# Graph 0's two aggregations in plain fp32, its loads split over two queues

## The reference

```python
def _L0(x, adj):  return adj @ (x @ weight) + bias
def _L1(x, adj):                 # first 25 nodes only, five node groups
    for g, idx in enumerate(GROUPS):
        h = graph_conv(x[:, idx], adj[:, idx][:, :, idx], W1[g], b1[g])      # relu(norm_adj @ (x @ W) + b)
        fused[:, idx] += norm_w[g] * graph_conv(h, adj_g, W2[g], b2[g])
def _L2(x, adj):                 # h = x @ W.T + b; e, f = h @ a1, h @ a2
    u = adj * exp(e[:, :, None] + f[:, None, :] + a_b)
    return (u / u.sum(2)) @ h
x = layernorm(x + _L0(x, adj))
x = layernorm(x + _L1(x, adj))
x = layernorm(x + _L2(x, adj))
x = layernorm(x + _L3(x, adj))   # convolutions, message passing with exp(-dist), a gated unit
```

## Time and profile before

| | us |
|---|---|
| median of 3 runs | 573.02 |
| lowest, highest | 571.81, 573.85 |
| the profiled execution, its own time | 571.94 |
| its span in the trace | 570.2 |
| mean granted clock of TensorE | 0.998 |
| busy: PE, DVE, ACT, POOL | 550.7, 477.9, 399.0, 218.5 |

### The profile page before, as it was taken

How to read it: one execution, slowest core, us unless ns; L and a number is a source line. 1 busy time by engine, 2 the same in 40 slices (tenths; PEclk the granted TensorE clock), 3 DMA queues, 4 the chain that set the end, 5 groups by cost and what they waited for, 6 DMA issues and landing times.

```text
span 570.2 us, 12148 instructions
## 1 busy us (share of the span) xinstructions
PE 550.7 (97%) x3639; PEld 486.2 (85%) x3639; DVE 477.9 (84%) x1768; ACT 399.0 (70%) x844; POOL 218.5 (38%) x213
## 2 busy tenths in 40 slices
PE   6889999999999999999999999999999999999994
PEld 6777898989889898989898898989898988989684
DVE  3887778898888989888888889898888888898665
ACT  2477576777787868687777878686777778786452
POOL 3312125263534434352635344343526353442010
PEclk9999999999999999999999999999999999999999
DMA  7980060020020303030200203030302002000000
GB/s 182 327 281 1 1 202 1 2 79 36 20 93 0 111 0 111 0 111 0 80 32 24 87 0 111 0 111 0 111 0 89 23 23 88 2 20 20 2 20 18
DMA packets 33301, 34.46 MB, mean 60 GB/s; under 512 B 1663, under 2 KB 22531, under 8 KB 33146
## 3 DMA queue, kind: packets, MB, share of 16 engines
q1 hardware_dynamic: 32930, 33.99, 18.8%
q10 hardware_dynamic: 344, 0.15, 0.1%
HBM read 29.74 MB, written 4.39 MB: 60 GB/s over the span
## 4 chain that ended last, share of the span: by engine, by line
PE 86%; DVE 1%; ACT 1%; issue 0%; POOLq 0%; POOL 0%; DVEq 0%
PE bank L265 14%; PE bank L267 14%; PE bank L266 14%; PE pair L265 6%; PE pair L267 6%; PE pair L266 6%; PE bank L1685 5%; PE bank L1696 3%; PE bank L1789 2%; PE pair L1845 2%; PE pair L1777 2%; PE bank L1880 2%; PE bank L1881 2%; PE bank L1884 2%; PE bank L1750 1%; PE bank L1860 1%
## 5 line engine op out<-in xcount | busy, mean ns | idle before, releaser
L1173 POOL TENSOR_TENSOR rs<-ve,neg_half 128x4 f32<-128x4 f32 (+1 forms) x60 | 55.3, 921 | 136.1 <-DVE ve L1409 101.2
L1207 POOL TENSOR_TENSOR P_lo<-P,P_hi 128x512 fp32r<-128x512 f32 x56 | 81.9, 1482 | 49.0 <-ACT P_hi L1246 49.0
L265 PE MATMUL bank<-cd_hi,w_hi 128*128 128x256 f32 x272 | 77.2, 284 | 0.0
L266 PE MATMUL bank<-cd_lo,w_hi 128*128 128x256 f32 x272 | 76.5, 281 | 0.0
L267 PE MATMUL bank<-cd_hi,w_lo 128*128 128x256 f32 x272 | 76.2, 280 | 0.0
L1444 DVE TENSOR_TENSOR P<-bank,aT 128x512 f32<-128x512 f32 x64 | 41.1, 684 | 16.7 <-ACT bank L1232 16.6
L265 PE MATMUL pair<-aT_hi,x_hi 128*128 128x512 f32 x128 | 52.2, 408 | 1.5 <-DVE x_lo L809 1.3
L266 PEld LDWEIGHTS bank<-cd_lo,w_hi 128*128 128x128 f32 x272 | 51.2, 188 | 1.6
L265 PEld LDWEIGHTS bank<-cd_hi,w_hi 128*128 128x128 f32 x272 | 51.3, 189 | 1.4
L267 PEld LDWEIGHTS bank<-cd_hi,w_lo 128*128 128x128 f32 x272 | 51.4, 189 | 0.0
L267 PE MATMUL pair<-aT_hi,x_lo 128*128 128x512 f32 x128 | 50.5, 394 | 0.0
(11 more groups left out here) (384 smaller groups left out, 1695.7 us busy)
## 6 DMA issues: line engine op xcount, KB each, us to landing
adj_nat<-in_adj_dram SPq DMA_DIRECT2D x16, 1024.0 KB, 5.9
x_nat<-in_x_dram SPq DMA_DIRECT2D x16, 256.0 KB, 2.9
xt<-in_x_dram SPq DMA_DIRECT2D x3, 1280.0 KB, 12.2
out_dram<-y_out SPq DMA_DIRECT2D x15, 256.0 KB, 2.3
hw<-in_L_gnn_W_dram SPq DMA_DIRECT2D x2, 640.0 KB, 8.4
xt<-in_L_gnn_conv_w_dram SPq DMA_DIRECT2D x1, 1088.0 KB, 6.8
aT<-in_adj_dram SPq DMA_DIRECT2D x5, 96.0 KB
nat_ih<-in_L_gnn_w_ih_dram SPq DMA_DIRECT2D x1, 384.0 KB, 6.1
```

Of the source, the lines that this page charges most:

```text
L265: nc.tensor.matmul(o, lh, rh, start=start, stop=False)
L266: nc.tensor.matmul(o, lh, rl, start=False, stop=False)
L1173: g.tensor_tensor(rs[i][:, 0:n], ve[i][:, 0:n], neg_half[:, 0:n], ALU.pow).then_inc(po_rs[i], 1)
L1207: g.tensor_tensor(P_lo[:, mc, :], P[:, mc, :], f(P_hi[:, mc, :]), ALU.subtract).then_inc(po_Plo[mc], 1)
```

## The change

Both aggregations of graph 0 take unsplit fp32 operands in one product for each chunk instead of three passes; copies, rests and their waits go (semaphores that the loop counts on are raised by hand). Adjacency 0 comes in two halves of two chunks, and TensorE transposes the first half of every block, then the second. The own-row loads wait for the first half. `xt` 0 to 2, `hw1` and `hw2` are issued by ScalarE, the first two after the first half has landed, the last three behind the four adjacency copies; four vectors move to SyncE, and SyncE's loads of own rows of x wait for `xt` 1. On TensorE the output product comes ahead of `transpose_rows`, and the latter are spread out. On VectorE, own-row masks of tile 1 move behind y1's statistics, those of tile 2 behind the normalisation.

```diff
@@ sync
-                sp.dma_start(adj_nat[0][:, :, :], adj_v[0]).then_inc(adj_in[0], 16)
+                sp.dma_start(adj_nat[0][:, 0:2, :], adj_v[0][:, 0:2, :]).then_inc(q_adj0, 16)
+                sp.dma_start(adj_nat[0][:, 2:NC, :], adj_v[0][:, 2:NC, :]).then_inc(adj_in[0], 16)
+                sp.wait_ge(q_adj0, 16)
...
-                sp.wait_ge(adj_in[0], 16)
-                x_tile(0)
-                sp.dma_start(hw1 ...)
+                for row, name, n in ((G2, ...), (BB2, ...), (M2, ...), (V2, ...)):
+                    sp.dma_start(vrows[row:row + n, :], ...)
...
-                sp.dma_start(hw2 ...)
-                x_tile(1)
-                x_tile(2)
+                sp.wait_ge(q_xr[1], 16)
@@ scalar
-                act.wait_ge(x_in[0], 16)
-                s.activation(x_hi[:, :, :], x_nat[0][:, :, :], ACT.Identity).then_inc(ac_xhi, 1)
+                act.sem_inc(ac_xhi, 1)
...
+                act.wait_ge(q_adj0, 16)
+                x_tile(0)
+                act.dma_start(hw1[:, :, :], ...).then_inc(q_h1, 16)
                 for mc in range(NC):
                     act.wait_ge(pe_aT[mc], 1)
-                    s.activation(aT_hi[:, mc, :], bank[mc][:, :], ACT.Identity).then_inc(q_aThi, 1)
+                    s.activation(aT[0][:, mc, :], bank[mc][:, :], ACT.Identity).then_inc(ac_aT[mc], 1)
+                act.dma_start(hw2[:, :, :, :], ...).then_inc(q_h2, 16)
+                x_tile(1)
+                x_tile(2)
                 act.wait_ge(pe_agg1, 1)
                 s.activation(agg_sb[:, :], AG_BANK[:, :], ACT.Identity).then_inc(ac_agg1, 1)
                 copy_rows(0)
+                act.wait_ge(q_cols, 1)
+                s.activation(cols[:, :], bank[7][:, 0:NROWS], ACT.Identity).then_inc(q_colsb, 1)
                 copy_rows(1)
-                for mc in (2, 0, 1, 3):
...
-                    act.wait_ge(dv_aTlo[mc], 1)
-                    s.activation(aT[0][:, mc, :], bank[mc][:, :], ACT.Identity).then_inc(ac_aT[mc], 1)
...
-                    s.activation(x_hi[:, c, 1:D], x2[:, c, 1:D], ACT.Identity, scale=pef[:, 1, c:c + 1])...
+                    s.activation(x3[:, c, 1:D], x2[:, c, 1:D], ACT.Identity, scale=pef[:, 1, c:c + 1])...
@@ vector
-                v.tensor_tensor(x_lo[:, :, :], x_nat[0][:, :, :], f(x_hi[:, :, :]), ALU.subtract).then_inc(x_rest, 1)
+                dve.sem_inc(x_rest, 1)
                 for mc in range(NC):
-                    rest_of_adjacency(mc)
-                dve.wait_ge(adj_in[0], 16)
+                    dve.sem_inc(dv_aTlo[mc], 1)
+                dve.wait_ge(q_adj0, 16)
...
                 degrees(NODES, 0, NG, 1)
-                dve.wait_ge(q_adjP, 32 * PJ)
-                v.tensor_tensor(AB[0:R, 1:NT, :], ...).then_inc(q_A1, 1)
-                hold(dve, q_A1, 3)
-                mask_blocks(1)
                 inverse_degrees(NODES, 0, NG, 1)
...
-                mask_blocks(2)
+                dve.wait_ge(q_adjP, 32 * PJ)
+                v.tensor_tensor(AB[0:R, 1:NT, :], ...).then_inc(q_A1, 1)
+                hold(dve, q_A1, 3)
+                mask_blocks(1)
...
+                mask_blocks(2)
                 mask_blocks(3).then_inc(q_A5, 1)
...
-                v.tensor_copy(x_hi[:, :, 0], pef[:, 1, :]).then_inc(dv_pfh, 1)
-                dve.wait_ge(dv_pfh, 1)
-                v.tensor_tensor(x_lo[:, :, 0], pef[:, 1, :], f(x_hi[:, :, 0]), ALU.subtract).then_inc(dv_pf, 1)
+                v.tensor_copy(x3[:, :, 0], pef[:, 1, :]).then_inc(dv_pf, 1)
+                dve.sem_inc(dv_pfh, 1)
                 for c in range(NC):
-                    hold(dve, ac_xs[c], 1)
-                    v.scalar_tensor_tensor(x_lo[:, c, 1:D], ...).then_inc(dv_xs[c], 1)
+                    dve.sem_inc(dv_xs[c], 1)
@@ tensor
+                def aggregate(mc):
+                    pe.wait_ge(ac_aT[mc], 1)
+                    last = t_.matmul(AG_BANK[:, :], x_nat[0][:, mc, :], aT[0][:, mc, :], start=(mc == 0), stop=(mc == NC - 1))
...
+                pe.wait_ge(q_adj0, 16)
+                for mc in range(NC):
+                    for c in range(2):
+                        t_.transpose(bank[mc][:, ch(c)], adj_nat[0][:, c, ch(mc)], ident[:, :])
                 pe.wait_ge(adj_in[0], 16)
                 for mc in range(NC):
-                    for c in range(NC):
+                    for c in range(2, NC):
                         last = t_.transpose(bank[mc][:, ch(c)], adj_nat[0][:, c, ch(mc)], ident[:, :])
                     last.then_inc(pe_aT[mc], 1)
                 pe.wait_ge(q_gm, 2)
-                pe.wait_ge(ac_xhi, 1)
-                pe.wait_ge(x_rest, 1)
-                for mc in range(NC):
-                    pe.wait_ge(dv_aTlo[mc], 1)
-                    last = three(pe, AG_BANK[:, :], x_hi[:, mc, :], x_lo[:, mc, :], aT_hi[:, mc, :], aT_lo[:, mc, :],
-                                 mc == 0, mc == NC - 1)
-                last.then_inc(pe_agg1, 1)
-                pe.wait_ge(q_adjP, 32 * PJ)
-                transpose_rows(0)
-                transpose_rows(1)
+                aggregate(0)
+                aggregate(1)
+                aggregate(2)
+                aggregate(3)
...
+                pe.wait_ge(q_adjP, 32 * PJ)
+                transpose_rows(0)
                 pe.wait_ge(q_row, 16 * 14)
-                pe.wait_ge(q_aPT, 2)
...
-                transpose_rows(2)
+                transpose_rows(1)
                 own_sums(0)
...
                 last.then_inc(q_hid0, 1)
+                transpose_rows(2)
...
-                    pe.wait_ge(dv_xs[mc], 1)
-                    last = three(pe, AG_BANK[:, :], x_hi[:, mc, :], x_lo[:, mc, :], aT_hi[:, mc, :], aT_lo[:, mc, :], ...)
+                    pe.wait_ge(ac_aT[mc], 1)
+                    last = t_.matmul(AG_BANK[:, :], x3[:, mc, :], aT[0][:, mc, :], ...)
```

More of the change, by code:

```diff
@@ L348, in _ @@
                         sp.dma_start(adjP[NODES * j + lo:NODES * j + hi, :, :], rows[j, lo:hi]).then_inc(q_adjP, 16)
-                def x_tile(t):
-                    sp.dma_start(xt[t][:, :, :, :].rearrange("p j c d -> p j (c d)"),
-                                 a["x"][1 + PJ * t:1 + PJ * (t + 1)].rearrange("j (p c) d -> p j (c d)", p=128)).then_inc(q_xr[t], 16)
-                sp.wait_ge(adj_in[0], 16)
-                x_tile(0)
-                sp.dma_start(hw1[:, :, :], a["L1_gnn_W1"].rearrange("g i h -> i g h")).then_inc(q_h1, 16)
+                for row, name, n in ((G2, "L3_gnn_bn2_g", 1), (BB2, "L3_gnn_bn2_b", 1), (M2, "L3_gnn_bn2_m", 1),
+                                     (V2, "L3_gnn_bn2_v", 1)):
+                    sp.dma_start(vrows[row:row + n, :], a[name].rearrange("(n d) -> n d", n=n)).then_inc(q_row, 16)
                 sp.wait_ge(q_zero, 1)
@@ L506, in _, with x_tile @@
                 act.dma_start(vrows[HB:BMSG, :], a["L1_gnn_b1"].rearrange("g (h d) -> (g h) d", h=2)).then_inc(q_row, 16)
+                def x_tile(t):
+                    act.dma_start(xt[t][:, :, :, :].rearrange("p j c d -> p j (c d)"),
+                                  a["x"][1 + PJ * t:1 + PJ * (t + 1)].rearrange("j (p c) d -> p j (c d)", p=128)).then_inc(q_xr[t], 16)
+                act.wait_ge(q_adj0, 16)
+                x_tile(0)
+                act.dma_start(hw1[:, :, :], a["L1_gnn_W1"].rearrange("g i h -> i g h")).then_inc(q_h1, 16)
                 for mc in range(NC):
                     act.wait_ge(pe_aT[mc], 1)
-                    s.activation(aT_hi[:, mc, :], bank[mc][:, :], ACT.Identity).then_inc(q_aThi, 1)
+                    s.activation(aT[0][:, mc, :], bank[mc][:, :], ACT.Identity).then_inc(ac_aT[mc], 1)
+                act.dma_start(hw2[:, :, :, :], a["L1_gnn_W2"].rearrange("g (h p) o -> p g h o", h=2)).then_inc(q_h2, 16)
+                x_tile(1)
+                x_tile(2)
                 act.wait_ge(pe_agg1, 1)
@@ L544, in _ @@
                 for c in range(NC):
-                    s.activation(x_hi[:, c, 1:D], x2[:, c, 1:D], ACT.Identity, scale=pef[:, 1, c:c + 1]).then_inc(ac_xs[c], 1)
+                    s.activation(x3[:, c, 1:D], x2[:, c, 1:D], ACT.Identity, scale=pef[:, 1, c:c + 1]).then_inc(ac_xs[c], 1)
                 def scale_taps():
@@ L702, in _ @@
                                 spread(deg[0:NODES, 3, 0:NG], NODES), ALU.mult).then_inc(q_nT, 1)
-                mask_blocks(2)
+                dve.wait_ge(q_adjP, 32 * PJ)
+                v.tensor_tensor(AB[0:R, 1:NT, :], adjP[0:R, :, 0:NODES], bc(EY[0:R], PT), ALU.add).then_inc(q_A1, 1)
+                hold(dve, q_A1, 3)
+                mask_blocks(1)
                 hold(dve, po_rs[0], 1)
@@ L966, in transpose_second @@
                     last.then_inc(pe_aT[mc], 1)
+                def aggregate(mc):
+                    pe.wait_ge(ac_aT[mc], 1)
+                    last = t_.matmul(AG_BANK[:, :], x_nat[0][:, mc, :], aT[0][:, mc, :], start=(mc == 0), stop=(mc == NC - 1))
+                    if mc == NC - 1:
+                        last.then_inc(pe_agg1, 1)
```

(5 more changed lines are left out.)

18 lines of the change are left out of this document (3 added, 15 removed).

## The result

The changed kernel takes 581.39 us (median of 4 runs, 580.23 to 583.37), the kernel before in the same comparison 572.41: ratio 1.016, interval 1.0134 to 1.0186, +9.0 us. Predicted were +2.7 and at most 578.2; the time is outside the range, on the side forecast. The profiled execution of the changed kernel was its slowest (583.37, span 581.6), the one of before near its lowest (571.94), so this pair of traces shows +11.4, and what follows accounts for those. TensorE's mean granted clock was 0.979 in the two longest executions of the changed kernel (583.37, 582.08) and 0.985 in the two shortest.

The account below looks back on a forecast made before the run. The first 68 us, ending in a barrier that moves with line 1068, were taken to decide. Hold +2.4, masks +1.45, second aggregation -1.1 gave +2.7: 575.7 us on the median; range 573.8 to 577.8, with rivals 571.2 to 578.2.

Parts of the forecast that it names:

- ScalarE held by x_tile(1) and x_tile(2): First block: their issues delay ScalarE's copy of the sum from 16.59 to 19.0 (17.0 to 21.0), 2.4 us later.
- The remaining 3.35 at 314 takes 10.7 us: 18.7: ScalarE's queue: of 4.8 MB to move before release, 3.35 MB remain after 8 us, moving at 314 GB/s.
- poor case: ScalarE's queue: 174 GB/s as in 8 to 12 us first, 314 after, so release at 20.4.
- the price of +2.4: Copy of the sum on ScalarE: starts 2.4 us later than 16.59 because of the held issues.
- TensorE's clock: Rival: idle from about 15.0 to 19.6, TensorE runs at 1.2 GHz up to the hidden layer; +2.5 us, 578.2, chance 0.07.
- Masks behind y1: VectorE: own rows' AB and first masked blocks move behind y1, making the degree chain 1.45 us later.
- Second aggregation: Without rests x1P comes 1.2 us sooner and line 1068 at 42.8 for 43.97; gain 1.1 us (0.5 to 1.2).
- First aggregation: TensorE: four fp32 products take 3.6 us against 3.0, ending at 14.7 to 15.3 against 16.5.
- The rest: Four vectors on SyncE, more adjacency copies on ScalarE, SyncE's wait for x_tile(1) ahead of xP: cost nothing.
- Issue time: ScalarE's load issues: not small as the skill page says; by its rule three issues would cost about 1.3 us.

Follow-up runs that it names:

- experiment 1: Changed kernel with hw2, x_tile(1) and x_tile(2) issued by SyncE behind the biases instead of by ScalarE; 578.41 us, ratio 1.0094.
- experiment 3: Kernel before with only hw2, x_tile(1) and x_tile(2) issued by ScalarE ahead of the copy of the sum; 574.81 us, ratio 1.0042.
- experiment 11: Changed kernel with ScalarE waiting for the own rows' adjacency before it issues x_tile(0), hw1 and what follows; 582.76 us, ratio 1.0173.
- experiment 7: Changed kernel with 86 dummy transposes on TensorE between the fourth aggregation product and its wait for the copy; 579.54 us, ratio 1.0118.
- experiment 2: Changed kernel with 70 dummy transposes on TensorE between the fourth aggregation product and its wait for the copy; 580.75 us, ratio 1.0114.
- experiment 5: Changed kernel with all five large loads on SyncE in the order of before, the four vectors issued by ScalarE again; 573.56 us, ratio 1.0007.
- experiment 10: Kernel before with only VectorE's order changed: own rows' AB and block 1 masks behind y1, block 2 masks behind x2; 574.16 us, ratio 1.0019.
- experiment 6: Experiment 5's kernel with VectorE's order of before: own rows' AB and block 1 masks ahead of y1; 575.12 us, ratio 1.0044.
- experiment 8: Kernel before with only the second aggregation in fp32, four products instead of twelve, no rests; 570.91 us, ratio 0.9977.
- experiment 9: Kernel before with both aggregations in fp32, loads and VectorE's order kept; 571.68 us, ratio 0.9977.
- experiment 4: Changed kernel with all five large loads on SyncE in the order of before, the four vectors still on SyncE; 577.90 us, ratio 1.0071.

## Why the prediction was wrong

- *ScalarE held by x_tile(1) and x_tile(2)*: that it is held is right (rows of ScalarE above; experiments 1 and 3). The step that failed is the size of the hold, "The remaining 3.35 at 314 takes 10.7 us: 18.7". The amount was good: predicted were 4.8 MB moved when ScalarE is let go, and up to 23.2 the changed kernel moved 188 GB/s x 7.6 + 222 x 9.8 + 168 x 5.8 us, or 4.6 MB (the first rate from the same view, 0 to 7.6). The rate was not: 202 GB/s on the mean from 7.6 on. The 314 came from a stretch of before in which only loads to 128 partitions moved. In the changed kernel the own rows' loads, to 9 or 16 each, were on SyncE's queue beside large ones on ScalarE's. The prediction's poor case used 174 GB/s for 4 us only; experiment 11 has them at 112 for 8.5. The copy's 4.2 us beyond the forecast are the largest part of what is missing. Where the order of the loads stays, the price of +2.4 holds; that the copy also fell on 18.86 there was in part luck, for TensorE was late (experiment 3) and only 4.2 MB had moved. When exactly an issue returns is not settled. By the packets of ScalarE's queue, x_tile(1)'s issue came back in the changed kernel with 1.0 MB of that queue still ahead of it and x_tile(2)'s with 1.7, in experiment 3 with 0.7 and 1.9 (an estimate, sizes less bytes moved); the prediction had read 0.7 and 1.5 out of before.
- *TensorE's clock*, a rival given 0.07 and 2.5 us, came true, and on top of the hold: 0.9 us in the product and 2.8 in the hidden layer in the profiled pair, 2.4 by the ratios (experiment 7). The only row it was measured against was TensorE's 2.27 us without a fall. Experiment 2 had a fall after 2.17, so that row proved nothing. The passage cited from the Trainium skill, "TensorE: Matmul & The Clock Gate", section "HAM oscillation — how this bites in real kernels", was the better guide: the changed kernel's trace agrees with it, granted clock 0.50 from 17.4 after TensorE's last work at 14.41. Experiment 5's fall, below, is not behind such a wait.
- *Masks behind y1*: 1.45 predicted, 1.72 in the profile, 1.1 by the ratio of experiment 10 (0.2 to 2.0). Right as long as the own rows are early; where they are late the move gains 2.1 (experiment 6, the clock's share in it), which the prediction did not see.
- *Second aggregation*: -1.1 predicted. Alone it gives -1.3 by the ratio (experiment 8; 0.4 to 2.2); the changed kernel's profile has 1.0 of it between exp(f) and x1P, and loses 0.7 again at the wait for `v`. The prediction put nothing on the last row transposes behind the hidden layer. All five profiled executions with this order and the hidden layer at 1.2 GHz have the wait (0.8 us; 1.7 in experiment 5), and so has experiment 6's at 2.4 GHz; those of 7 and 11 do not.
- *First aggregation*: 3.6 us for four products (3.60 and 3.67) is right, the end at 14.41 even ahead of 14.7 to 15.3. Without the hold that start would have been won: experiment 5 copies the sum at 13.91. Even so that kernel is in the median no faster than before, and experiment 9, with it, no faster than 8 without.
- *"The rest" at nothing*: right in the changed kernel, where the four vectors are issued behind ten small loads only; wrong in experiment 4, where they have x_tile(0) ahead of them.
- *Issue time.* The page "DMA: Bandwidth & Descriptors" of the Trainium skill, section "Issuing engines are not separate DMA queues", counts issue time as usually small. Here two issues took 12.0 us of ScalarE, so the measurement decides for the row. That a second issuing engine buys no bandwidth agrees with 202 GB/s on two queues for 254 on one (7.6 to 20.1 in before).

The sum for the profiled pair: hold 6.6, product 0.9, masks 1.7, hidden layer 2.8, wait for `v` 0.7, second aggregation -1.0: 11.7 at line 1068, 11.4 at the end.

Experiment 5, with the loads of before and 2.7 us of head start, is 1.7 us above experiments 8 and 9 in the median. That goes with the clock: where its mean was 0.995 or more, experiment 5 took 570.9 in the median, experiment 8 570.6 and experiment 9 571.3. Nine of experiment 5's twelve executions were below that, three of experiment 9's twelve. What stays open is why this order loses the clock so often.

## What to carry to other kernels

Before a load is issued from an engine that also computes, add up what is still queued ahead of it: the issue itself can hold the engine until a part of that has moved (here it returned with 0.7 to 1.9 MB still ahead), and everything behind it in program order waits. Take the rate for that sum from a stretch in which the same kinds of loads move, not from the best stretch. And price a stand of TensorE twice, once for its length and once for the work behind it at half the clock; filling it with dummy work kept the clock in all four executions when the fill reached nearly to the end of the stand (experiment 7), and in two of four when it was some 2 us too short (experiment 2). And compare executions by their mean granted clock before reading a median.

## What was not expected of the hardware

- The clock fell without a long stand. Experiment 5's profiled execution, TensorE from 16 to 24 us, and two windows of it:

```profile
16.97 0.74 PE L875 MATMUL bank<-ident,aT 125*128 125x125 f32 x4 [0.28 <-DMA aT<-in_adj_dram]
17.64 0.48 PE L997 MATMUL bank<-ident,vrows 28*128 28x128 f32 x2
18.47 0.99 PE L875 MATMUL bank<-ident,aT 125*128 125x125 f32 x4 [0.35 <-ACT cols L517]
20.23 1.93 PE L901 MATMUL bank<-xt,aPT 128*32 128x128 f32 x32 [0.76 <-ACT aPT L445]
...
23.29 4.56 PE L1010 MATMUL bank<-U,hw 128*128 128x100 f32 x20 [0.41 <-issue]
```

```profile
16.00:19.00 3.00, 2.37 (x17) 1.83 (x16) 2.54 (x14) 0.67 (x2) 0.69 (x1) 0.96 0.97 336
19.00:32.00 13.00, 11.10 (x72) 9.21 (x71) 7.63 (x56) 2.91 (x9) 3.76 (x3) 0.50 1.08 346
```

  No stand is over 0.8 us, and the clock was at 1.2 GHz for some 13 us, with TensorE busy 85% of them. Other executions of this kernel were up to 4.7 us shorter (575.26 with a mean clock of 0.984 for this one, 570.54 with 0.996 for the shortest). What tips it is not known.
- Busy DMA engines are no measure of bytes: share 1.14 at 168 GB/s, 1.01 at 345, in the windows above.
- fp32 products of 128x512 cost 0.90 us each at 2.4 GHz, for three passes of rounded operands at about 0.23 us apart, 0.7 in all; the three-pass form wins only what its rests don't take back.
